# Cross attention with a returned bundle: text probabilities and sums turned by the transfers that turn the probabilities, in two halves, and queries made per batch

## The reference

```python
q = (x @ Wq).reshape(B, N, HEADS, DIM_HEAD)
k = (ctx_txt @ Wk).reshape(...); v = (ctx_txt @ Wv).reshape(...)
out = _attend(q, k, v)              # softmax(q k^T * SCALE) v, per head
k_ip = (ctx_img @ Wk_ip).reshape(...); v_ip = (ctx_img @ Wv_ip).reshape(...)
out = out + _attend(q, k_ip, v_ip)
return out @ Wo + bo
```

## Time and profile before

| | us |
|---|---|
| median of 3 runs | 2439.89 |
| lowest and highest run | 2439.25, 2445.34 |
| the profiled execution | 2435.73 (span 2433.6) |
| PE busy in it | 2160.2 (89%) |
| DVE, ACT, POOL busy | 1570.4 (65%), 925.0 (38%), 877.5 (36%) |
| cross attention, first to last row maximum (L2449) | 628.8 to 2005.4 |

### The profile page before, as it was taken

The page is one execution under the profiler, slowest core; times in us unless marked ns, Lnnn a source line. Parts: engine busy times, 40 slices in busy tenths (PEclk is TensorE's granted clock), DMA queues, the critical chain, the costliest instruction groups (busy, mean ns, idle before and its releaser), DMA issues. The chain is left out here.

```text
span 2433.6 us, 37422 instructions
## 1 busy us (share of the span) xinstructions
PE 2160.2 (89%) x13637; PEld 1726.1 (71%) x13637; DVE 1570.4 (65%) x2756; ACT 925.0 (38%) x1869; POOL 877.5 (36%) x535
## 2 busy tenths in 40 slices
PE   5878877796699999999999999999999997787897
PEld 3445545464598889888898998998998994334684
DVE  4179934333577677677677677777776763795554
ACT  1166611210244344344344444444443443452331
POOL 1066412431343333243343333343333300362455
PEclk8989977798899999999999999999999998798898
DMA  5800002511476677677676777776776656001364
GB/s 159 169 16 14 8 1 88 230 50 57 145 200 184 185 218 205 185 217 206 185 217 180 226 202 208 198 207 199 202 211 186 194 156 248 4 0 44 98 148 114
DMA packets 229957, 362.99 MB, mean 149 GB/s; under 512 B 41920, under 2 KB 197824, under 8 KB 225168
## 3 DMA queue, kind: packets, MB, share of 16 engines
q1 hardware_dynamic: 223008, 342.08, 48.1%
q0 software_dynamic: 6768, 18.49, 3.2%
HBM read 234.97 MB, written 125.50 MB: 148 GB/s over the span
## 5 line engine op out<-in xcount | busy, mean ns | idle before, releaser
L2271 PE MATMUL img_ps<-cn,pt_hi 128*128 128x256 f32 (+1 forms) x3072 | 569.7, 287 | 3.0 <-DVE pt_lo L2478 3.0
L2271 PEld LDWEIGHTS img_ps<-cn,pt_hi 128*128 128x128 f32 (+1 forms) x3072 | 477.3, 191 | 3.2 <-issue 3.2
L2271 PE MATMUL img_ps<-cn,pt_lo 128*128 128x256 f32 (+1 forms) x1536 | 435.9, 284 | 0.0
L2466 DVE STREAM_TRANSPOSE prob_blocks<-prob 128x384 f32<-128x384 f32 x512 | 250.6, 547 | 183.8 <-ACT prob L2402 175.9
L2248 PE MATMUL s_ps<-ct,a_hi 128*128 128x508 f32 x768 | 315.7, 411 | 0.0
L2249 PE MATMUL s_ps<-ct,a_hi 128*128 128x508 f32 x768 | 304.2, 396 | 0.0
L2250 PE MATMUL s_ps<-ct,a_lo 128*128 128x508 f32 x768 | 304.0, 396 | 0.0
L2001 POOL TENSOR_SCALAR ct<-staged 128x762 fp32r<-128x762 f32 x64 | 136.8, 2138 | 439.6 <-DMA staged<-in_ctx_t 312.5
L2271 PEld LDWEIGHTS img_ps<-cn,pt_lo 128*128 128x128 f32 (+1 forms) x1536 | 292.6, 190 | 0.0
L2478 DVE TENSOR_TENSOR pt_lo<-prob_moved,pt_hi 128x768 fp32r<-128x768 f32 x256 | 277.9, 1124 | 9.4 <-ACT pt_hi L2414 9.2
L2001 POOL TENSOR_SCALAR cn<-staged 128x768 fp32r<-128x768 f32 x64 | 137.4, 2147 | 376.5 <-DMA staged<-in_ctx_n 293.4
(11 more groups left out here) (370 smaller groups left out, 3712.9 us busy)
## 6 DMA issues: line engine op xcount, KB each, us to landing
prob_rows<-prob_blocks SPq DMA_DIRECT2D x512, 192.0 KB, 2.1
prob_moved<-prob_rows SPq DMA_DIRECT2D x512, 192.0 KB, 3.6
staged<-in_ctx_n SPq DMA_DIRECT2D x64, 384.0 KB, 4.7
staged<-in_ctx_t SPq DMA_DIRECT2D x64, 381.0 KB, 4.7
up_all_m<-in_up SPq DMA_DIRECT2D x8, 2048.0 KB, 12.8
down_all_m<-in_down SPq DMA_DIRECT2D x8, 1024.0 KB, 23.4
sums_m<-y_b SPq DMA_DIRECT2D x63, 128.0 KB, 2.2
w_shared<-in_wq SPq DMA_DIRECT2D x7, 1024.0 KB, 7.3
```

What stands on the lines that cost most here:

```text
L2271: last = nc.tensor.matmul(img_ps[:, 0:D], left[0:n, j, :], rows[0:n, right, j, :], start=j == 0 and at == 0, stop=j == IB - 1 and at == 2)
L2466: nc.vector.transpose(blocks[:, m], source[:, m]).then_inc(turned, 1)
```

## The change

- `prob` gets three more blocks of 128 columns: one for the normed text probabilities and two for the scaled sums. DVE turns all fifteen blocks, now in two instructions of 960 columns instead of four of 384; SP stores them in two transfers of 480 KB with 3840 contiguous bytes per partition, and reads them back in four of 240 KB (two for each half).
- Text and sums of step g-3 travel with the image probabilities of step g (`LAG = 3`). `turn_text`, `turn_sums` and their copies go; `value_side(g-4)` runs in iteration g and reads `moved` directly, behind a wait for bundle g-1. There are two more iterations of the loop at its end.
- `moved` has one buffer, so bundle g is read back only when pt_lo of step g-1 is made and `value_side(g-4)` is copied out.
- `sums`: pt_hi is multiplied by both parts of cn in one matmul of 512 columns into the whole bank, pt_lo by part 0 into its second half: 24 matmuls instead of 36. ACT scales the second half into `o_part`, and DVE adds it while it scales the first (SCALAR_TENSOR_TENSOR).
- The text's exponentials go to `txt_prob`; ACT norms them, not DVE.
- `queries(b)` makes one batch (32 fp32 matmuls of 64 columns) at the end of the 7th and 14th step of a tile; ACT alone copies them. key_side no longer moves behind the sums. `project` comes in the fifth step of a tile, ahead of the sums.
- wq and wo are loaded in halves of 512 KB: wq at steps 4 and 5 of a tile, for the queries at the end of step 6; wo at steps 14 and 15.

```diff
-        block_rows = nc.dram_tensor("prob_rows", (2, Q, P, RUN), F32).ap()
-        moved = [sb(f"prob_moved{s}", [P, Q, IB, QR]) for s in range(2)]
+        block_rows = nc.dram_tensor("prob_rows", (2, PARTS, P, PQ, RUN), F32).ap()
+        moved = sb("prob_moved", [P, Q, BUNDLE, QR])
...
+            return {6: 2 * i + 1, 13: 2 * i + 2 if i < NT - 1 else None}.get(n) if g < N else None
...
-            for g in range(N):
+            for g in range(N + LAG):
                 if g >= 2:
-                    sp.wait_ge(moved_in[s], 16 * Q * (g // 2))
+                    sp.wait_ge(moved_in, 16 * Q * (g - 1))
+                for u in range(PARTS):
+                    sp.wait_ge(turned, PARTS * g + u + 1)
+                    sp.dma_start(block_rows[s, u].rearrange("p m f -> p (m f)"),
+                                 blocks[:, quarters(u)].rearrange("p m j r -> p (m j r)")).then_inc(stored[u], 16)
+                if g:
+                    sp.wait_ge(split_done, 2 * min(g, N))
+                if g > LAG:
+                    sp.wait_ge(valued, g - LAG)
                 for m in range(Q):
-                    sp.wait_ge(turned, Q * g + m + 1)
-                    sp.dma_start(block_rows[s, m], blocks[:, m].rearrange("p j r -> p (j r)")).then_inc(stored[m], 16)
-                if g >= 2:
-                    sp.wait_ge(split_done, 2 * (g - 1))
-                for m in range(Q):
-                    sp.wait_ge(stored[m], 16 * (g + 1))
...
+                    if m % PQ == 0:
+                        sp.wait_ge(stored[m // PQ], 16 * (g + 1))
+                    sp.dma_start(moved[m * QR:(m + 1) * QR].rearrange("c a j r -> c a (j r)"),
+                                 block_rows[s, m // PQ, :, m % PQ].rearrange("(a c) f -> c a f", a=Q)).then_inc(moved_in, 16)
...
+                if n in (4, 5) and i:
+                    sp.wait_ge(projected, i)
+                    sp.dma_start(wq[:, n - 4], src["wq1"][:, n - 4]).then_inc(wq_in, 16)
...
-                        for at, (left, right) in enumerate(((pt_hi, 0), (pt_hi, 1), (pt_lo, 0))):
-                            last = nc.tensor.matmul(img_ps[:, 0:D], left[0:n, j, :], rows[0:n, right, j, :],
-                                                    start=j == 0 and at == 0, stop=j == IB - 1 and at == 2)
+                        nc.tensor.matmul(img_ps[:], pt_hi[0:n, j, :], rows[0:n, :, j, :], start=j == 0, stop=False)
+                        last = nc.tensor.matmul(img_ps[:, D:2 * D], pt_lo[0:n, j, :], rows[0:n, 0, j, :],
+                                                start=False, stop=j == IB - 1)
...
+                pe.wait_ge(moved_in, 16 * Q * (g + LAG + 1))
...
-                        nc.tensor.matmul(out, wv[:, c, cols], ot[:, c, rows], start=c == 0, stop=False)
+                        nc.tensor.matmul(out, wv[:, c, cols], moved[:, rows, O_AT + c, :], start=c == 0, stop=False)
...
+                if projects(g) is not None:
+                    project(projects(g), head_place)
                 if 2 <= g <= N + 1:
                     sums(g - 2)
...
+                if LAG + 1 <= g <= N + LAG:
...
+                    value_side(g - LAG - 1)
+                    head_place = ring.place(1)
+                if queries_of(g) is not None:
+                    if g >= STEPS:
+                        pe.wait_ge(wq_in, 32 * (g // STEPS) + 16)
+                    q_place = queries(queries_of(g))
...
+                    nc.scalar.activation(o_part[:], img_ps[:, D:2 * D], ACT.Copy,
+                                         scale=inv[(g - 2) % 3][:, 1:2]).then_inc(part_kept, 1)
+                    act.wait_ge(turned, PARTS * min(g + 1, N + LAG))
+                    nc.scalar.activation(prob[:, TXT_AT * P:TXT_AT * P + TXT], txt_prob[(g - 2) % 3][:], ACT.Copy,
+                                         scale=inv[(g - 2) % 3][:, 0:1]).then_inc(txt_normed, 1)
...
+                    nc.vector.scalar_tensor_tensor(out=prob[:, O_AT * P:], in0=img_ps[:, 0:D],
+                                                   scalar=inv[(g - 2) % 3][:, 1:2], in1=o_part[:], op0=ALU.mult,
+                                                   op1=ALU.add).then_inc(sums_kept, 1)
```

More of the change, by code:

```diff
@@ L2209, in kept, with queries @@
                 pe.wait_ge(t_kept[place[0]], place[1])
-            def queries(t):
-                for side in range(2):
-                    bank = use()
-                    for j in range(4):
-                        p = 4 * side + j
-                        for c in range(C):
-                            last = nc.tensor.matmul(t_ps[bank][:, j * P:(j + 1) * P], wq[:, c, p * P:(p + 1) * P],
-                                                    k.h_t[:, c, t * P:(t + 1) * P], start=c == 0, stop=c == C - 1)
-                    last.then_inc(t_done[bank], 1)
-                return ring.place(2), ring.place(1)
+            def queries(b):
+                bank = use()
+                for p in range(PAIRS1):
+                    for c in range(C):
+                        last = nc.tensor.matmul(t_ps[bank][:, p * S:(p + 1) * S], wq[:, c, p * P:(p + 1) * P],
+                                                k.h_t[:, c, b * S:(b + 1) * S], start=c == 0, stop=c == C - 1)
+                last.then_inc(t_done[bank], 1)
+                return ring.place(1)
             def key_side(g):
@@ L2311, in _ @@
             pe.wait_ge(wq_in, 16)
-            q_places = queries(0)
+            q_place = queries(0)
             pe.wait_ge(wk_in, 16)
-            for place in q_places:
-                kept(place)
+            kept(q_place)
             a_place = key_side(0)
-            for g in range(N + 3):
+            for g in range(N + LAG + 2):
                 if g < N:
@@ L2355, in flat @@
             return a[:].rearrange("p c n -> p (c n)")
-        def keep_queries(eng, copy, mine, ring):
-            for side in range(2):
-                bank, count = ring.next()
-                if side == mine:
-                    eng.wait_ge(t_done[bank], count)
-                    for r in range(2):
-                        rows = slice(r * HD1, (r + 1) * HD1)
-                        last = copy(q[rows, 4 * side:4 * side + 4, :, r, :],
-                                    t_ps[bank][rows, :].rearrange("p (j b n) -> p j b n", j=4, b=2))
-                    last.then_inc(t_kept[bank], 1)
         def by_block(tile, h):
@@ L2386, in keep_a, with keep_queries @@
                 nc.scalar.activation(flat(a_hi), t_ps[bank][:, 0:D], ACT.Copy).then_inc(a_hi_kept, 1)
+            def keep_queries(b):
+                bank, count = ring.next()
+                act.wait_ge(t_done[bank], count)
+                act.sem_inc(queried, 1)
+                for r in range(2):
+                    rows = slice(r * HD1, (r + 1) * HD1)
+                    last = copy(q[rows, :, b % 2, r, :], t_ps[bank][rows, :].rearrange("p (j n) -> p j n", j=PAIRS1))
+                last.then_inc(t_kept[bank], 1)
             act.wait_ge(q_zeroed, 1)
-            keep_queries(act, copy, 0, ring)
+            keep_queries(0)
             keep_a(0)
-            for g in range(N + 3):
-                if 1 <= g <= N:
-                    keep(act, copy, ring, pt_txt[(g - 1) % 3][0:TXT, :], TXT, P)
-                if g >= 3:
-                    keep(act, copy, ring, flat(ot), P, D)
-                if not boundary(g) and g < N - 1:
+            for g in range(N + LAG + 2):
+                if g < N - 1:
                     keep_a(g + 1)
+                if projects(g) is not None:
+                    ring.next()
+                    ring.next()
                 if g < N:
@@ L2440, in _ @@
             nc.vector.memset(q[:], 0.0).then_inc(q_zeroed, 1)
-            dve.wait_ge(q_zeroed, 1)
-            keep_queries(dve, copy, 1, ring)
-            dve.sem_inc(queried, 1)
+            ring.next()
             keep_a_lo(0)
             dve.wait_ge(pad_zeroed, 1)
-            for g in range(N + 3):
+            for g in range(N + LAG + 2):
                 if g < N:
@@ L2453, in _ @@
                     nc.vector.tensor_scalar(bias[g % 2], top[g % 2], -SCALE, None, ALU.mult).then_inc(bias_done, 1)
[L2454 to L2466 removed]
+                if g < N - 1:
+                    keep_a_lo(g + 1)
```

191 lines of the change are left out of this document (81 added, 110 removed).

## The result

The changed kernel takes 2570.2 us (median of 4 runs, 2561.6 to 2588.3) where the kernel before takes 2440.1 on the same chip: a ratio of 1.054, with a 95% interval of 1.048 to 1.060. I had predicted 2435, in a range of 2403 to 2482. It is 130 us slower, and 88 us above my range.

What follows compares the result with a forecast made beforehand. TensorE's work bounded the kernel; VectorE, transfers and one wait would follow. Terms -31 -46.5 +52.5 -8 +13 -4 +4 +1.5 +14 sum to -4.5 us: 2431 from the profiled 2435.7, plus 4.2 for the median, 2435; range 2403 to 2482.

Steps and rivals of the forecast that it cites:

- TensorE's own step: TensorE's work in a cross-attention step: 10.11 less 0.32 for turning matmuls and 0.11 for wide sums, giving 9.68 us.
- The new wait: Value side waits for the last bundle: two steps need 19.7 us, a step 9.86; 125 plain steps give -31 us.
- The stores don't add: Stores are issued 1.0 and 2.0 us ahead of pt_lo's end and take 1.9, so they do not lengthen the wait.
- Queries: Two sets a tile of 32 matmuls with 64 columns, 3.5 us a set; fifteen sets in the loop: +52.5 us.
- the old boundary's price: Seven old tile boundaries, 6.6 us each for queries, waiting and smaller gaps; removing them gives -46.5 us.
- the wait for wq: TensorE idle 1.8 us, seven times, for wq's second half ahead of a query set: +13 us, between 0 and 20.
- insertions hide part of themselves: Each of 22 insertions (15 query sets, 7 projections) hides up to 0.35 us in TensorE's slack: -8 us.
- Ends: Start of the kernel +1.5 us; tail, with three returns in a row, 40 us against 28.3 before: +14 (9 to 18).
- The first: Rival, chance 0.22: TensorE stays the bound, steps of 9.68 us, about -21 us in all, 2419.
- The second: Rival, chance 0.25: POOL's two-input subtraction gets ahead of pt_lo, a step is 10.3 us, +52 on the forecast, 2487.
- The third: Rival, chance 0.08: queries run by columns or wq lands in time, 15 to 23 us less than forecast, about 2415.
- The single `moved` buffer orders nothing more in a plain step: Claim that the one buffer for returned bundles adds no further ordering in a plain step; no cost counted.

Runs made afterwards that it cites:

- e12: Kernel of e11 plus the change's wide sums (512 columns of pt_hi in one matmul, low half scaled by ScalarE, added by VectorE): 2435.0 us, ratio 0.998.
- e1: Changed kernel, but the value side multiplies an unchanging piece of wk and so waits for no bundle: 2495.4 us, ratio 1.020.
- e3: Changed kernel with two buffers for returned bundles, text values loaded once, and a value side that waits for nothing: 2469.7 us, ratio 1.011.
- e5: Changed kernel, but each return brings back only the twelve image blocks (192 KB); the stores stay at fifteen: 2469.0 us, ratio 1.011.
- e6: Changed kernel with POOL's second instruction for each context piece taking one input in place of two: 2563.7 us, ratio 1.051.
- e9: Changed kernel with two bundle buffers, text values loaded once, a value side that waits for nothing, and no wq reload or wait for it: 2426.9 us, ratio 0.995.
- e7: Changed kernel, but from the third batch each staged context piece brings 64 columns (32 KB) in place of some 0.5 MB: 2545.2 us, ratio 1.043.
- e8: Kernel before with only the change's two waits (returns for last step's pt_lo, TensorE for the last bundle before each value side): 2461.3 us, ratio 1.009.
- e4: Changed kernel without the reload of wq in steps 4 and 5 of a tile and without the wait for it: 2552.1 us, ratio 1.045.
- e2: Changed kernel with two buffers for returned bundles and text values loaded once; the value side still waits for the last bundle: 2543.0 us, ratio 1.040.
- e11: Kernel before, with the next step's key side run between the two halves of the sums at a tile's end, not behind them: 2441.8 us, ratio 1.001.
- e14: Kernel of e12 with VectorE's half of the query copies ahead of its four turning instructions at a tile's end: 2417.3 us, ratio 0.990.

## Why the prediction was wrong

**TensorE's own step** was 9.68 and is 9.75. The turns gave their 0.32 at most, and the wide sums not 0.11 but 0.04 to 0.08 (e12). Here the rule I had set against my rows was the nearer one: the Trainium skill's 2.5 ns for each matmul joined away (TensorE: Matmul & The Clock Gate, "Back-to-back issue gap", which gives it for isolated matmuls) makes an estimate of 0.03 us a step. Both are small.

**The new wait** is the step that failed. That TensorE would wait there for the bundle was right. What failed is the length of the chain, and that I saw one chain where there are two:

| term, us | predicted | measured (median) |
|---|---|---|
| scores to turning | 8.43 | 8.46 |
| two turning instructions | 2.2 | 2.24 |
| scores to the first return's issue | 12.65 | 14.1 |
| landing to end of pt_lo | 3.25 | 3.47 |
| pt_lo to issue | 0.15 | 0.03 |
| four returns | 6.45 | 6.81 |
| first store landed, from scores | 12.4 | 13.3 |
| two steps | 19.7 | 21.6 |

The issue of the first return came 1.45 us late, most of the 1.9 that are missing. I let pt_lo start as soon as the turning was over, at 10.65. But it needs pt_hi of the last bundle, which in steps away from insertions has landed only at 9.7 to 10.0; its first half starts at 11.1 to 11.3 and its second ends at 13.5 to 13.8 (median and mean), where I had 12.5. So each late landing makes the next return late. "The single `moved` buffer orders nothing more in a plain step" is therefore wrong: by my own terms its round was 3.25 + 0.15 + 6.45 = 9.85 us, as long as my step, and it measured 10.2 to 10.3; with the value side's wait gone it still held plain steps at 10.05 (e1 against 9.75 in e3). What lengthened both chains:

1. The returns: the increment for the bytes was right (+0.8, measured 0.92 by e5), the base was not. I took 5.65 from one quiet step; over all steps of the kernel before the median is 5.83 and the mean 5.95.
2. "The stores don't add": a store of 480 KB takes 3.3 us to land, not the 1.9 of 192 KB. With pt_lo's end at my 12.5 the store would have been last.
3. pt_lo: POOL's first instruction, which I had not counted, makes a half 1.57 instead of 0.95, and this befell 80 of the 256 halves of the changed kernel, and 3 before. The earlier trace rows showed only the second instruction. The Trainium skill names both (SBUF — State Buffer, "Who interferes with whom": a Vector instruction with two SBUF inputs contends with any GpSimd instruction that reads SBUF), and e6, where both of POOL's instructions have one input and both still stretch it, agrees.

All three went the same way, and I had 0.25 us of room. The upper bound I gave to a step, 10.16, was itself below what came.

**What a wait costs** was the missing term. I priced idle time at its length; here it brings TensorE's clock down, and it falls to 1.2 GHz again and again. By the table above the changed kernel holds 85 us more idle time than e9 and loses up to 55 us more to the clock; the 127 steps differ by 135. The runs show when. Waits of over 0.65 us between 700 and 1970 us, in the changed kernel and e1 to e3, e5 to e7 together: where a query set followed, the scores behind it ran slow (over 4.8 us instead of 4.48) after 67 of 77; where none followed, after 39 of 156, and after none of the 62 among them that were shorter than 1.2 us. That last is not a rule: in e8, four of 14 such shorter waits had slow scores behind them. In e4, which is not in the count either, it was 4 of 6 and 12 of 31. In e9, where no wait precedes a set, all 15 sets of the loop ran at full clock.

**Queries:** 3.5 us a set was right (13.33 - 9.75 = 3.58 in every run), and so was the old boundary's price. The 47 us over my 56 are the value side's wait and the wait for wq (mine: 1.8 each, measured 1.3 to 1.6), followed by the lower clock: the step of the first set takes 18.6, that of the second 15.2. That insertions hide part of themselves was right in sign (e1's projections take 12.55, not 13.27), and worth little.

**Ends:** the tail is 49.2 us, 21 more than before, not 14 more:

```profile
L2469 DVE TENSOR_TENSOR x_sb<-x_sb,t_ps x16: 261/276/288, 888.4 to 2165.6; 128x128 f32<-128x128 f32 x16
```

with returns of about 7 us where I had 5.5 to 6. The head is 6 longer; in the runs of the changed kernel's kind it is 14.3 to 17.5, by the clock of its first query set (from its first matmul to the key side 8.5 us in the changed kernel, e2 and e7, 5.2 to 6.4 in the others), and ScalarE copies the queries alone.

**Rivals.** The first (TensorE stays the bound; its terms add up to about -23, not -21) is what e9 shows, but only without the waits. The second had the right sign and a step of 10.3, near the plain steps' median, by the wrong cause. The third is refuted: no set ran in 2 us. None of mine, and not the chances of 0.34 for slower, held 5%: I added the rivals to the forecast one at a time, while the late terms and the clock came together.

Not tried: the changed kernel with wo and wq in separate tiles. And why the clock fell in one wait of 1.2 to 1.7 us with a set behind it and not in another is open.

## What to carry to other kernels

When a change turns a transfer from something hidden into something waited for, take its time from the mean over all steps and not from one row, and ask what the engine's clock does behind the wait: here the 127 steps grew by 135 us for 85 us more of idle time, 1.6 for each. Two chains of nearly one length have to be shortened together (e1, e2, e3), and a repair is worth nothing until the last wait of its place is found (e11 against e14). Batching small data into a large transfer makes the small data as late as the large: the same blocks in returns of their own, read a step later, and one query set moved away from its wait turned +5.4% into -0.65%.

## What the hardware showed that I had not expected

- TensorE's clock falls more readily when a fp32 query set (32 matmuls of 64 columns, 3.5 us) follows a wait than when the scores do: 67 of 77 against 39 of 156. In the stretch shown, which has no set in it, the granted clock was 0.57. A load of 1 MB that came 2.3 us late cost 6 us a tile (e3 against e9). The Trainium skill names waits for transfers as a cause of a clock that goes up and down (TensorE: Matmul & The Clock Gate, "HAM oscillation — how this bites in real kernels"), and these runs agree.
- A one-input POOL instruction on SBUF stretches a two-input VectorE instruction from 0.95 to 1.57 us (80 of the 131 that began in it), and a two-input one to as much as 2.6 (ten of 23). The Trainium skill speaks of an exclusive lock on shared ports (SBUF — State Buffer, "Who interferes with whom"); the shorter stretch is not one that lasts: POOL's instruction had some 2.07 us left, and VectorE's took only 0.62 more. In most of these cases POOL's began during the first half of pt_lo, and was itself longer, 2.8 us instead of 2.13.
- Four returns on one queue take 6.81 us whether the load beside them has 384 or 32 KB, but 5.89 when they themselves are a fifth smaller.
